# Second softmax pass of two attention layers: weighted sums in runs of four steps, items of the next batch between the shifted scores

## The reference, cut to what matters

```python
# layer 0                                        # layer 1
q  = latents @ q_w + q_b                         a = layer_norm(audio_kv)
kv = concat([x, latents]) @ kv_w + kv_b          Q, K, V = h @ Wq.T, a @ Wk.T, a @ Wv.T
attn = where(mask, q @ k.T / DH, -inf)           attn = softmax(where(mask, Q @ K.T * scale, -inf))
out  = softmax(attn) @ v @ out_w + out_b + res   out  = h + tanh(gate) * (attn @ V) @ Wo.T
out  = gelu(rmsnorm(out) @ w1 + b1) @ w2 + b2 + res
```

## Time and the profile before

| | |
|---|---|
| median of three runs | 2562.28 us |
| the profiled execution, its own time | 2558.9 us |
| its span, first to last instruction | 2556.9 us |
| PE busy | 2434.6 us, 95% |
| ACT busy | 1498.4 us, 59% |
| DVE busy | 1200.0 us, 47% |
| mean granted TensorE clock | 0.982 |
| layer 0, from one second pass to the next | 66.52 us |
| layer 1, the same | 42.73 us |

### The profile page before, as it was taken

How to read it: one execution, slowest core, us unless ns; L and a number is a source line. 1 busy time by engine, 2 the same in 40 slices (tenths; PEclk the granted TensorE clock), 3 DMA queues, 4 the chain that set the end, 5 groups by cost and what they waited for, 6 DMA issues and landing times. The chain is left out here.

```text
span 2556.9 us, 43876 instructions
## 1 busy us (share of the span) xinstructions
PE 2434.6 (95%) x14656; PEld 1902.6 (74%) x14656; DVE 1200.0 (47%) x2350; ACT 1498.4 (59%) x3418; POOL 228.1 (9%) x260
## 2 busy tenths in 40 slices
PE   6999999999999999979999999999899999999998
PEld 5677777777777777658888888888677777777775
DVE  4455555555555555542222122112266565656564
ACT  3677777777777777753222222222267676767676
POOL 2000000000000000010000000000221212121210
PEclk8999999999999999989999999999899999999998
DMA  6343343334444443342111011012245454445442
GB/s 173 95 100 99 100 103 99 99 99 101 108 108 107 108 107 91 91 128 67 50 49 40 10 49 49 16 33 82 66 119 140 110 138 110 138 109 139 109 123 76
DMA packets 148186, 239.00 MB, mean 93 GB/s; under 512 B 25600, under 2 KB 59680, under 8 KB 148144
## 3 DMA queue, kind: packets, MB, share of 16 engines
q1 hardware_dynamic: 148144, 238.46, 34.8%
HBM read 86.28 MB, written 25.21 MB: 44 GB/s over the span
## 5 line engine op out<-in xcount | busy, mean ns | idle before, releaser
L532 ACT ACTIVATE l_score_ps<-l_score_ps,l_neg_max 128x512 f32<-128x512 f32 (+1 forms) x1024 | 567.4, 557 | 298.9 <-DVE l_neg_max L708 296.9
L708 DVE TENSOR_REDUCE l_neg_max<-l_score_ps 128x1 f32<-128x512 f32 (+1 forms) x768 | 490.5, 683 | 72.0 <-PE l_score_ps L949 71.7
L552 ACT ACTIVATE l_probs<-l_score_ps 128x1024 f32<-128x1024 f32 x384 | 386.3, 1019 | 92.8 <-PE l_score_ps L982 89.6
L1246 ACT ACTIVATE mlp_hidden<-mlp_hidden_ps,mlp_b_col 128x512 f32<-128x512 f32 x128 | 88.3, 690 | 496.1 <-PE mlp_hidden_ps L66 496.0
L949 PE MATMUL l_score_ps<-l_stack 97*128 97x512 f32 (+1 forms) x1024 | 319.8, 370 | 29.2 <-ACT l_score_ps L532 13.9
L1281 DVE TENSOR_TENSOR mlp_hidden_l<-mlp_hidden,mlp_hidden_h 128x512 fp32r<-128x512 f32 x128 | 95.1, 744 | 516.2 <-ACT mlp_hidden_h L1248 516.2
L982 PEld LDWEIGHTS l_score_ps<-l_stack 99*128 99x128 f32 x1536 | 210.3, 191 | 134.5 <-issue 81.0
L982 PE MATMUL l_score_ps<-l_stack 99*128 99x256 f32 x1536 | 273.7, 304 | 22.7 <-DVE l_qk L687 15.6
L997 PE MATMUL l_o_ps<-l_probs,l_v 128*32 128x256 f32 x3072 | 240.0, 392 | 1.8
L949 PEld LDWEIGHTS l_score_ps<-l_stack 97*128 97x128 f32 x1024 | 175.8, 194 | 76.8 <-ACT l_score_ps L532 41.9
L728 DVE TENSOR_TENSOR l_o_norm<-l_o_ps,norm_room 128x256 f32<-128x256 f32 x128 | 54.4, 425 | 357.9 <-PE l_o_ps L997 357.9
(11 more groups left out here) (136 smaller groups left out, 4282.4 us busy)
## 6 DMA issues: line engine op xcount, KB each, us to landing
l_stack<-room SPq DMA_DIRECT2D x256, 192.0 KB
l_stack<-l_qk SPq DMA_DIRECT2D x256, 128.0 KB
l_stack<-room SPq DMA_DIRECT2D x128, 128.0 KB
l_stack<-l_qk SPq DMA_DIRECT2D x256, 64.0 KB
l_tokens<-in_x SPq DMA_DIRECT2D x16, 512.0 KB, 4.0
l_tokens<-in_ctx SPq DMA_DIRECT2D x16, 512.0 KB, 4.9
l_stack<-room SPq DMA_DIRECT2D x128, 64.0 KB
l_rows<-in_x SPq DMA_DIRECT2D x16, 512.0 KB, 3.3
```

What stands on the lines that cost most here:

```text
L532: m = act.activation(e, e, ACT.Exp, bias=neg_max[:, q, h:h + 1], accum_out=row_sum[:, q, h:h + 1])
L552: act.activation(probs[:, s % PROBS, :].rearrange("p (a b) -> p a b", a=2), score_ps[:, 2 * (s % 2):2 * (s % 2) + 2, :], ACT.Exp).then_inc ...
L708: dve.tensor_reduce(out, bank, AXIS_X, ALU.max, negate=True).then_inc(max_done, 1)
L1246: act.activation(hidden[:, m % HBUF, :], hidden_ps[m % 4][:, :], ACT.Gelu_apprx_tanh, bias=b1_col[:, m:m + 1])
```

## The change

The second pass is rebuilt, and the first pass gives items and steps to it.

- PE: the last items (layer 0: K3, Q0, Q1; layer 1: K3) leave the slots. K3 is made in four quarters with shifted steps 0, 1, 2 and `turn_shift(1)`, `spread_sums(1)` between them; in layer 0 Q0 and Q1 stand later, with one shifted step in the middle of each. `weigh` comes in runs of four (`run(r)`), 4 runs in layer 0 and 2 in layer 1.
- Layer 0: the first AHEAD = 4 score steps of batch p stand at the end of the second pass of a. Both layers: the first quarter of one v block of batch p (`v_ahead`) stands before `project(3)`.
- The step tables are new, TURN_SLOT is the second item slot after T3 (K1), the second half is turned in the second pass; `weigh_norm` of layer 0 stands ahead of the maximum of its slot.
- ACT and DVE have the new order; in layer 1 `layer_norm_stats` and `layer_norm` stand among the normalisations.
- PROBS is 5. `dynamic_dma_scratch_size=8192` is given. SP issues the mask row first and then waits and moves the stack.

```diff
-    PROBS = 3
+    PROBS = 5
...
+    MIXED = NT + NK - 1
+    SLOT = [("share", 0)] + [("v", t) for t in range(PLAIN_V)] + [("item", k) for k in range(MIXED)]
     SLOTS = len(SLOT)
-
-    STEPS_AT_FIRST = [0, 0, 0, 2, 3, 3, 4, 4, 4, 4, 4, 4, 0] if first else [0, 1, 1, 2, 2, 4, 4, 2, 0]
-    STEPS_IN_SLOT = [2, 4, 2, 2, 1, 1, 1, 4, 4, 4, 4, 3, 0] if first else [2, 1, 1, 1, 2, 3, 3, 3, 0]
+    RUN = 4
+    AHEAD = RING if first else 0
+    STEPS_AT_FIRST = [0, 0, 4, 4, 4, 4, 4, 4, 4, 4] if first else [0, 0, 2, 2, 2, 3, 4, 3]
+    STEPS_IN_SLOT = [2, 4, 4, 1, 1, 1, 3, 4, 4, 4] if first else [0, 0, 2, 2, 2, 3, 3, 4]
     AFTER_T = SLOT.index(("item", NT))
-    TURN_SLOT = [AFTER_T + (3 if first else 1), SLOTS - 1]
-    SPREAD_SLOT = TURN_SLOT[0] + 1
-    SQUARE_SLOT, SCALE_SLOT, NORM_SLOT = 1, 3, AFTER_T + 1
+    TURN_SLOT = AFTER_T + 1
+    SPREAD_SLOT = TURN_SLOT + 1
+    SQUARE_SLOT, SCALE_SLOT, NORM_SLOT = 1, 3, AFTER_T
...
+        def load_stacks(sp, b, half, lows):
...
+            sp.dma_start(f32(stack[MASK_ROW:MASK_ROW + 1, HALF * half:HALF * (half + 1), K_COLS]),
+                         mask_rows[bass.ds(b, 1), :].rearrange("o (h k) -> o h k", h=1).to_broadcast([1, HALF, KEYS])
+                         ).then_inc(stack_loaded[half], 16)
+            sp.wait_ge(low_done, lows)
...
+            def second_pass_of_two_keys(p, a):
+                exps(a, 0)
+                copy_shift(a, 1)
+                exps(a, 1)
+                exps(a, 2)
+                copy_inv(a, 1)
+                exps(a, 3)
+                if p is not None:
+                    high(p, MIXED)
+                o_high(a, 0)
+                exps(a, 4)
+                o_high(a, 1)
+                exps(a, 5)
+                exps(a, 6)
+                exps(a, 7)
+                o_high(a, 2)
+                o_high(a, 3)
+            def second_pass_of_four_keys(p, a):
+                exps(a, 0)
+                copy_shift(a, 1)
+                exps(a, 1)
+                exps(a, 2)
+                copy_inv(a, 1)
+                exps(a, 3)
+                if p is not None:
+                    high(p, MIXED)
+                exps(a, 4)
+                if p is not None:
+                    high(p, MIXED + 1)
+                exps(a, 5)
+                exps(a, 6)
+                o_high(a, 0)
+                exps(a, 7)
+                if p is not None:
+                    high(p, MIXED + 2)
+                exps(a, 8)
+                exps(a, 9)
+                exps(a, 10)
+                o_high(a, 1)
+                exps(a, 11)
+                exps(a, 12)
+                exps(a, 13)
+                exps(a, 14)
+                o_high(a, 2)
+                exps(a, 15)
+                o_high(a, 3)
+                if p is not None:
+                    for k in range(AHEAD):
+                        step_sum(p, k)
...
+                    if first and prev is not None and slot == NORM_SLOT + 1:
+                        weigh_norm(prev)
...
+                norm_next = not first and p is not None and not (isinstance(p, int) and p == B - 1)
+                make_shift(a, 1)
+                if first:
+                    if p is not None:
+                        low(p, MIXED)
+                        low(p, MIXED + 1)
+                    normalise(a, 0)
+                    o_low(a, 0)
+                    if p is not None:
+                        low(p, MIXED + 2)
+                    normalise(a, 1)
+                    o_low(a, 1)
+                else:
+                    normalise(a, 0)
+                    if p is not None:
+                        low(p, MIXED)
+                    o_low(a, 0)
+                    normalise(a, 1)
+                    if norm_next:
                         layer_norm_stats(p + 1)
-                if not first and p is not None and not (isinstance(p, int) and p == B - 1):
-                    layer_norm(p + 1)
-                if a is not None:
-                    for g in range(FB):
-                        normalise(a, g)
-                        o_low(a, g)
-                    finish(a)
+                    o_low(a, 1)
+                    if norm_next:
+                        layer_norm(p + 1)
+                normalise(a, 2)
+                o_low(a, 2)
+                normalise(a, 3)
+                o_low(a, 3)
+                if p is not None:
+                    for k in range(AHEAD):
+                        step_max(p, k)
+                finish(a)
...
+            def v_ahead(b):
+                pe.wait_ge(low_done, ITEMS * (b + 1))
+                pe.wait_ge(o_norm_done, FB * b - 1)
+                v_passes(b, PLAIN_V, 0)
...
+            def items_free(p):
+                if p is not None:
+                    pe.wait_ge(low_done, ITEMS * (p + 1))
+            def second_pass_of_two_keys(p, a, run):
+                run(0)
+                shifted(a, 4)
+                shifted(a, 5)
+                items_free(p)
+                project(a, 0)
+                shifted(a, 6)
+                shifted(a, 7)
+                project(a, 1)
+                run(1)
+                project(a, 2)
+            def second_pass_of_four_keys(p, a, run):
+                halves = itertools.count()
+                def between(s):
+                    if next(halves) == 2:
+                        shifted(a, s)
+                if p is not None:
+                    item(p, a, MIXED + 1, lambda: between(4))
+                else:
+                    shifted(a, 4)
+                run(0)
+                shifted(a, 5)
+                shifted(a, 6)
+                halves = itertools.count()
+                if p is not None:
+                    item(p, a, MIXED + 2, lambda: between(7))
+                else:
+                    shifted(a, 7)
+                shifted(a, 8)
+                run(1)
+                shifted(a, 9)
+                shifted(a, 10)
+                items_free(p)
+                project(a, 0)
+                shifted(a, 11)
+                shifted(a, 12)
+                run(2)
+                shifted(a, 13)
+                shifted(a, 14)
+                project(a, 1)
+                shifted(a, 15)
+                run(3)
+                project(a, 2)
+                if p is not None:
+                    for k in range(AHEAD):
+                        scores(p, k)
...
+                quarter = itertools.count()
+                def between():
+                    q = next(quarter)
+                    if q >= 1:
+                        shifted(a, q - 1)
+                    if q == 2:
+                        turn_shift(a, 1)
+                    if q == 3:
+                        spread_sums(a, 1)
+                def run(r):
+                    for s in range(RUN * r, RUN * (r + 1)):
                         weigh(a, s)
-                        if s >= KB and s % KB == KB - 1 and s < PSTEPS - 1:
-                            project(a, s // KB - 1)
-                    for g in range(FB - 2, FB):
-                        project(a, g)
+                if p is not None:
+                    item(p, a, MIXED, between)
+                else:
+                    pe.wait_ge(v_copied, KB * (a + 1))
+                    for _q in range(FB):
+                        between()
+                shifted(a, 3)
+                if first:
+                    second_pass_of_four_keys(p, a, run)
+                else:
+                    second_pass_of_two_keys(p, a, run)
+                if p is not None:
+                    v_ahead(p)
+                project(a, 3)
...
-    nc = bacc.Bacc("TRN2", target_bir_lowering=False, num_devices=1)
+    nc = bacc.Bacc("TRN2", target_bir_lowering=False, num_devices=1, dynamic_dma_scratch_size=8192)
```

More of the change, by code:

```diff
@@ L19 @@
 from concourse import mybir
+import itertools
 from contextlib import ExitStack
@@ L271, in steps_of @@
         def steps_of(slot, a):
-            counts = STEPS_AT_FIRST if isinstance(a, int) and a == 0 else STEPS_IN_SLOT
-            return range(sum(counts[:slot]), sum(counts[:slot + 1]))
+            at_first = isinstance(a, int) and a == 0
+            counts, begun = (STEPS_AT_FIRST, 0) if at_first else (STEPS_IN_SLOT, AHEAD)
+            return range(begun + sum(counts[:slot]), begun + sum(counts[:slot + 1]))
         def v_bank(t):
@@ L581, in iteration @@
                     if a is not None:
-                        for half in range(HALVES):
-                            if TURN_SLOT[half] == slot - 1:
-                                copy_shift(a, half)
+                        if TURN_SLOT == slot - 1:
+                            copy_shift(a, 0)
                         if SPREAD_SLOT == slot - 1:
@@ L598, in iteration @@
                 if a is not None:
-                    for s in range(PSTEPS):
-                        exps(a, s)
-                        if s == 1:
-                            copy_inv(a, 1)
-                        if s >= KB and s % KB == 1:
```

(30 more changed lines are left out.)

38 lines of the change are left out of this document (9 added, 29 removed).

## The result

The kernel after takes 2538.84 us (median of four runs, 2537.15 to 2540.27), the kernel before on the same chip 2561.82 (2559.35 to 2572.01): 23 us less, a ratio of 0.9908 with a 95% interval of 0.9885 to 0.993. The forecast was 2502, 60 less. The sign is right and 2538.84 lies inside the range; the gain is 0.4 of the one forecast. The two profiled spans, 2556.9 and 2537.1, differ by 19.8.

What follows compares the result with a forecast made beforehand. PE's queue was taken to set the time. Savings of 4.5 and 4.15 us less added waits left 1.9 and 1.95 a batch; over 14 batches, plus 6 at the ends, 60 us off: 2502 us, range 2462 to 2547.

Steps and rivals of the forecast that it cites:

- The trip: On PE, entering and leaving a run of weighted sums costs 0.33 us; fewer runs save 3.3 us (layer 0), 1.65 (layer 1).
- The removed part: PE time saved through fewer runs and covered waits: 4.5 us a batch in layer 0, 4.15 in layer 1.
- Steps inside runs: On PE, each further weighted step inside a run costs 0.43 us.
- no wait for exponentials in a run's fourth step: Layer 0's second pass: exponentials ready 2.2 us before to 1.0 after run start; fourth step comes 1.4 in, so no wait.
- rival C: Layer 0's early head scores wait on SP's stack loads if issues run slower, up to 2581 us; forecast wait 0; chance 0.06.
- (a): Second pass: turn_shift(1) waits for last sum, K2's halves and make_shift(1): 1.3 us in layer 0, 1.2 in layer 1.
- (b): Slots with added score steps: layer 0's T1 and K0 waits cost 1.3 us net; layer 1's K0 first score 0.4 net.
- (c): Layer 1: project(2), right behind run 1, waits 0.6 us for normalise and output halves; layer 0's rest of pass: no wait.
- The ends: The two last batches save their trips, 3.3 + 1.65, and layer 0's last has four scores early, about 1: 6 us.
- B: ACT bounds layer 1, waits of (a) and (c) at upper bounds, layer 1 gains nothing: 2530 us; chance 0.22.
- A: All new waits covered as DVE and ACT catch up, so added costs vanish: 2435 us; chance 0.13 for below 2462.
- D: The trip isn't the tiling mode: steps inside long runs cost 0.57 like single ones: 2577 us; chance 0.04.

Runs made afterwards that it cites:

- e4: Kernel after with layer 0's first three runs of weighted sums and layer 1's first each cut in two around a shifted score: 2553.10 us.
- e19: e1 plus, in layer 0, all four maxima of the last slot ahead of low(K1) on DVE: 2514.53 us (one run).
- e2: Kernel after with copy_shift(0) on ACT after two of slot K1's four sums instead of after all four and high(K1): 2558.57 us.
- e1: Kernel after with make_shift(1) on DVE ahead of the low half of K2 instead of behind it, both layers: 2514.96 us, ratio to before 0.9789.
- e15: e1 plus, in layer 0, ACT's copies of v2 and v3 behind T3's sums instead of ahead of them: 2512.08 us (one run).
- e18: Probe on e1: POOL applies layer 1's gamma and beta to one column of each token row only: 2509.30 us (one run).
- run 0: Not a follow-up experiment: the first group of four weighted-sum steps on PE in a second pass, forecast in layer 0 at 8.5 us from K3's start.
- e17: e1 plus, in layer 1, the next batch's v_ahead ahead of project(2) instead of behind it: 2505.25 us (one run).
- e_all: Kernel after with e1's and e17's moves, layer 0's early copy_shift(0) and two maxima ahead of low(K1), one layer 1 step from K2 to T0: 2505.95 us.
- e129: e19 plus, in layer 0, copy_shift(0) after two of the sums of slot K1: 2507.14 us.

## Why the prediction was off

**What held.** The trip: 0.33 by e4 in layer 0. The removed part: 4.7 and 4.2 for 4.5 and 4.15 forecast. Steps inside runs at 0.43; no wait for exponentials in a run's fourth step in the middle batches. No wait of the head scores on the stack loads in the kernel after (rival C). That a change of tiling mode drains TensorE (the Trainium skill, "TensorEngine Tiling (Array Packing)", Tiling Modes, Key Properties) agrees with e4, which adds changes of mode and no work; the page gives no price.

**Where it failed: the costs of what was added.**

- (a), the wait for the second shift, was put at 1.3 and 1.2 us. PE loses 1.9 there in each layer (1.1 + 0.8 and 0.5 + 1.4). The term that was mis-sized is the end of the last sum: 1.8 us after K2's end in the forecast, 2.5 in layer 0 and 2.6 in layer 1 in the trace, which covers the missing 0.6 and 0.7. The prediction put the delay down to DVE's load in slot K1. But DVE stands idle there, 0.97 us in layer 0 and 1.12 in layer 1, ahead of low(K1). It waits for high(K1), which stands on ACT behind K1's sums, and three of the last slot's maxima stand behind low(K1). With these maxima ahead of it in layer 0 (e19) the last sum ends at 1.9.
- That the loss in (a) shows as two waits is a second step that failed. The prediction followed the chain of the second half of the shifts and not that of the first: copy_shift(0) on ACT and the shift rows' DMAs on SP were costed at nothing. In the kernel after this wait lies inside the time that (a) takes anyway (e2); once the second shift comes early (e1), it is what is left, 1.1 us in layer 0.
- (b), layer 0: 1.3 net forecast, 1.9 measured. K0's two scores wait 0.8 and 0.6, as forecast in size (0.7 each), though the copies of v ahead of T3's sums account for 0.2 us of it at most (e15). The missing 0.6 is T1: its wait for the copy of v was put at 0.4 and is 1.0. No run tried it. Layer 1: 0.4 net forecast, 0.5 measured.
- (c), layer 1: 0.6 forecast, 1.3 measured. The row for a DVE operation of 256 columns (0.43) was read in layer 0, where POOL was idle and the operation another one (L695). The kernel before's own rows beside POOL were 1.21 and 1.40. e18 gives the 0.6 back.
- The ends: 6 us forecast, about 0 measured (19.8 us of spans less the 19.7 of the middle batches). Their trips can't be priced as in the middle, because stretches at a granted clock of 0.50 lie across the last passes of both kernels: run 0 of layer 0's last pass takes 3.57 us there. What the trace of the kernel after shows besides is late exponentials between run 0 and run 1 of that pass, since no items stand between (0.64 and 0.27 us idle ahead of two shifted steps). Layer 1's last interval and pass are 0.4 and 0.6 us longer; how much of that is the clock is open.

In sum 14 x (1.07 + 1.37) + 6 = 40.2 us of gain didn't come, as much as the spans are short of the 60. (1.07 and 1.37 are the forecast gains of 1.9 and 1.95 a batch less the measured 0.83 and 0.58.)

**The rivals.** B (2530 us) is nearest in time, but by luck. It had layer 0 gain 1.9 us a batch and layer 1 nothing, and measured are 0.83 and 0.58. It had the waits at their upper bounds, and (a) is 1.9 against a bound of 3. Its mechanism, ACT as the bound, is wrong, since e1, e17 and e18 each won 0.6 to 0.8 us a batch without ACT doing less. A fell with every new wait. C and D fell as said.

**What stays open.** Why the clock falls in some batches of e2 and e_all and not in others with the same waits isn't settled. How much of K0's wait an earlier T2 sum would give back, and how much of T1's an earlier copy of v1, wasn't tried.

## What to carry to other kernels

When work is moved ahead of a step, follow each thing that the step waits for back to its engine's queue, the DMA rows and the buffers included, and not only the one that looks latest. Of waits in series toward one time, taking out an earlier one only makes the later one longer (e2). Ask what sets the common time and move that (e1 gave 22 us by the spans), and expect the next chain to end close behind it (e19 and e129 needed each other). An engine with much to do is not therefore late by its load: look for its idle time first. Read an operation's duration from a row of the same operation where the other engines do what they will do beside it.

## What the runs showed of the hardware

DVE's low half of layer 1 (L789, 128x256, l_o_norm and l_oT_h in) took 0.42 us alone and 1.05 beside POOL's multiplication, in the kernel before up to 1.40; `normalise` (L780, same size, one input in the bank l_o_ps) took 0.43 beside the same multiplication. Entering and leaving a run of 32-column matmuls cost PE 0.33 us (e4). The granted clock fell to 0.50 for about 3 us in single batches, after PE had stood idle 1.5 us of 3.7 (e2) and 1.1 of 2.0 (e_all), and each time cost 1.5 us: a short stall can cost more than its own length.
